# Projections turned before they leave the PSUM banks, stacks built by transfers through a scratch, keys and values by plain fp32 matmuls

## The reference, cut to what matters

```
Q = layernorm(x) @ Wq + bq ;  K = ctx @ Wk + bk ;  V = ctx @ Wv + bv
w = softmax(Q K^T * 0.25)               (32 heads, 4 of them share one key/value head)
x = x + tanh(g_xattn) * ((w V) @ Wo + bo)
x = x + tanh(g_ffn) * ffn(layernorm(x))     ffn: w1, w3 (512 -> 1792), silu, w2 (1792 -> 512)
```

## Time and profile before

| what | us |
|---|---|
| median of 3 runs (lowest to highest) | 392.64 (391.22 to 392.65) |
| the profiled execution: its own time | 391.85 |
| the profiled execution: span from first to last instruction | 390.1 |
| PE busy in the span | 377.4 |
| DVE, ACT, POOL busy in the span | 271.7, 209.1, 160.5 |

### The profile page before, as it was taken

How to read it: one execution, slowest core, us unless ns; L and a number is a source line. 1 busy time by engine, 2 the same in 40 slices (tenths; PEclk the granted TensorE clock), 3 DMA queues, 4 the chain that set the end, 5 groups by cost and what they waited for, 6 DMA issues and landing times.

```text
span 390.1 us, 6293 instructions
## 1 busy us (share of the span) xinstructions
PE 377.4 (97%) x2350; PEld 307.5 (79%) x2350; DVE 271.7 (70%) x452; ACT 209.1 (54%) x367; POOL 160.5 (41%) x135
## 2 busy tenths in 40 slices
PE   7789999999998999999999999999999999999996
PEld 5578888888887677878888888888888888888885
DVE  5978998979998967898776777543954344554334
ACT  4678999998999986552332332332332332332320
POOL 6558889898999785264333443000000000000000
PEclk9999999999999999999999999999999999999999
DMA  8903104100000040295000000000200000000002
GB/s 289 342 14 86 32 2 167 46 40 6 2 6 3 3 166 2 86 416 227 0 0 0 0 0 0 0 0 2 108 0 0 0 0 0 0 0 0 0 0 108
DMA packets 6817, 20.98 MB, mean 54 GB/s; under 512 B 875, under 2 KB 1131, under 8 KB 6668
## 3 DMA queue, kind: packets, MB, share of 16 engines
q1 hardware_dynamic: 6364, 19.92, 14.0%
q10 hardware_dynamic: 432, 0.79, 0.5%
HBM read 18.28 MB, written 2.10 MB: 52 GB/s over the span
## 4 chain that ended last, share of the span: by engine, by line
PE 83%; DVE 9%; DMA 3%; SPq 2%; ACT 1%; issue 1%; POOL 0%; DVEq 0%
PE ps L1767 23%; PE ps L1769 23%; PE ps L1768 22%; PE ps L1819 3%; PE ps L1809 3%; PE ps L1774 3%; DMA gsc<-in_small 3%; DVE MX L1142 2%; PE ps L1827 2%; PE ps L1775 1%; PE ps L1828 1%; DVE x2HL L1172 1%; DVE X L1183 1%; DVE aTL L1153 1%; DMA Qst<-Mrow 1%
## 5 line engine op out<-in xcount | busy, mean ns | idle before, releaser
L1767 PE MATMUL ps<-x2HL,w13H 128*128 128x512 f32 x224 | 89.1, 398 | 0.0
L1769 PE MATMUL ps<-x2HL,w13L 128*128 128x512 f32 x224 | 88.6, 395 | 0.0
L1768 PE MATMUL ps<-x2HL,w13H 128*128 128x512 f32 x224 | 88.4, 395 | 0.0
L340 POOL TENSOR_TENSOR PL<-E,PH 128x512 f16<-128x512 f32 x64 | 74.1, 1174 | 13.2 <-ACT E L609 7.2
L351 POOL TENSOR_TENSOR wres<-wres,gsc 128x1536 f32<-128x1536 f32 x14 | 42.5, 3037 | 44.2 <-DVE hf L1196 44.2
L632 ACT ACTIVATE T<-ps 128x512 f32<-128x512 f32 x28 | 16.7, 597 | 79.0 <-PE ps L1769 79.0
L640 ACT ACTIVATE hH<-hf 128x512 fp32r<-128x512 f32 x28 | 17.7, 632 | 63.5 <-DVE hf L1196 63.5
L1769 PEld LDWEIGHTS ps<-x2HL,w13L 128*128 128x128 f32 x224 | 42.0, 187 | 10.4
L1768 PEld LDWEIGHTS ps<-x2HL,w13H 128*128 128x128 f32 x224 | 42.0, 188 | 9.8
L1189 DVE SCALAR_TENSOR_TENSOR A<-T,ps 128x512 f32<-128x512 f32 x28 | 19.2, 685 | 43.8 <-ACT T L632 43.8
L1767 PEld LDWEIGHTS ps<-x2HL,w13H 128*128 128x128 f32 x224 | 42.0, 188 | 9.5
(11 more groups left out here) (112 smaller groups left out, 712.8 us busy)
## 6 DMA issues: line engine op xcount, KB each, us to landing
wres<-in_wff SPq DMA_DIRECT2D x14, 768.0 KB, 6.7
X<-in_x SPq DMA_DIRECT2D x8, 256.0 KB, 11.1
ct<-in_ctxt SPq DMA_DIRECT2D x7, 256.0 KB, 3.2
raw<-in_wproj SPq DMA_DIRECT2D x3, 512.0 KB, 6.3
out<-X SPq DMA_DIRECT2D x6, 256.0 KB, 2.0
raw<-in_wproj SPq DMA_DIRECT2D x1, 1024.0 KB, 9.4
Qst<-Mrow SPq DMA_DIRECT2D x32, 8.0 KB
out<-X ACTq DMA_DIRECT2D x2, 256.0 KB, 2.1
```

Of the source, the lines that this page charges most:

```text
L340: pool.tensor_tensor(PL[:, g % NL, :], E[:, g % NE, :], PH[:, g, :], ALU.subtract).then_inc(pL_ok, 1)
L1767: pe.matmul(out_ap, aH, bH, start=start, stop=False)
L1768: pe.matmul(out_ap, aH, bL, start=False, stop=False)
L1769: return pe.matmul(out_ap, aL, bH, start=False, stop=stop)
```

## The change

It does five things, and writes all five lists of operations anew.

1. **Keys and values** come from plain fp32 matmuls on the unsplit context `ct` and the unsplit weights `raw` (`project_kv32`): 4 matmuls of 256 columns for two batches at once, for K and for V each. The splits of the context (`context_high`, `context_low` on POOL) and of Wk, Wv are gone. The weights are the stationary operand, so that the result is turned: features on the partitions.
2. **Queries** too are made turned and for two batches at once: `project_q` for each j of 4, 4 x three matmuls of 256 columns.
3. **Biases** are then one value per partition and are added while the parts are written (`q_high`, `q_low`, `k_high`, `k_low`, `v_bias`); the bias matmuls are gone. V is turned back by `turn_v`.
4. **Stacks** are built by transfers: the high and low parts go to a scratch in device memory (`queries_out`, `keys_out`), and each of the three parts is read back from there to its 32 rows of `Qst` or `kst` (`queries_in`, `keys_in`). The 24 turns and 6 ACT copies per batch are gone. The score groups go by j instead of h, so `scores(n, j)` needs all four pairs.
5. **Maxima**: one transfer per batch (two for batch 0) into 16 rows, the sign moves into `sel`, `max_low` moves from DVE to POOL. The first layernorm's `normalise` moves from ACT to DVE (8), and 2 of the 8 of the second; some small steps (`epsilon`, `shift`) move to POOL, and the low part of Wq from DVE to POOL.

The diff, cut to its core:

```diff
-            def project_kv(n, bank, k):
-                project(bank, 2 * KVD, ctH[:, n % 2], ctL[:, n % 2], KV0, k)
-            def add_bias(bank, width, b0):
-                return pe.matmul(bank[:, 0:width], ones[:], brow[:, b0:b0 + width], start=False, stop=True)
-            def stack_k(h, bank):
-                for i in range(4):
-                    m = turn(bank[0:ROWS, i * P:(i + 1) * P], Ktok[...])
-            def stack_q(h, bank):
-                for j in range(GJ):
-                    m = turn(bank[0:ROWS, j * P:(j + 1) * P], Qtok[...])
+            def project_kv32(bank, n, w0, k0, k1):
...
+                for k in range(k0, k1):
+                    m = pe.matmul(bank[:, 0:TWO], raw[:, w0 + k * KVD:w0 + (k + 1) * KVD],
+                                  ct[:, n % NCT:n % NCT + 2, k * P:(k + 1) * P], start=k == 0, stop=k == KB - 1)
+            def project_q(bank, j, k0, k1):
+                for k in range(k0, k1):
+                    c = Q0 + (j // 2) * KB * TWO + k * TWO + (j % 2) * P
+                    w = slice(c, c + P)
+                    m = three(bank[:, 0:TWO], WpH[:, w], WpL[:, w], xTH[:, k, :, :], xTL[:, k, :, :], k == 0, k == KB - 1)
+            def turn_v(bank):
+                for b in range(2):
+                    m = turn(bank[:, b * P:(b + 1) * P], VT[:, b * P:(b + 1) * P])
```

```diff
+        qscr = nc.dram_tensor("qscr", [NBATCH // 2, 2, 2, P, GJ * P], F32).ap()
+        kscr = nc.dram_tensor("kscr", [NBATCH // 2, 2, P, 2, TWO], F32).ap()
+        def keys_out(eng, p, low):
+            eng.dma_start(kscr[p, low], r32((KTL if low else KTH)[:])).then_inc((kh_out, kl_out)[low], 16)
+        def keys_in(eng, p, t):
+            s = (NBATCH - NKST + 2 * p % NKST) * P
+            eng.dma_start(r32(kall(32 * t, 32 * t + 32)[:, :, s:s + TWO]),
+                         kscr[p, t % 2].rearrange("(r h) g n -> r (h g) n", h=PAIRS)).then_inc((k_in0, k_in1)[p % 2], 16)
+        def queries_out(eng, p, low, j0, j1, done):
+            eng.dma_start(qscr[p, low, :, :, j0 * P:j1 * P].rearrange("b r n -> r b n"),
+                         r32((QTL if low else QTH)[:, :, j0:j1, :]).rearrange("r b j q -> r b (j q)")).then_inc(done, 16)
+        def queries_in(eng, n, t, done):
+            eng.dma_start(r32(Qst[32 * t:32 * t + 32, n % 2, :, :]).rearrange("r h n -> r (h n)"),
+                         qscr[n // 2, t // 2, n % 2].rearrange("(r h) n -> r (h n)", h=PAIRS)).then_inc(done, 16)
+        def max_in(eng, n, j0, j1):
+            eng.dma_start(r32(Qst[ROWS:ROWS + NM, n % 2, :, j0 * P:j1 * P]),
+                         r32(Mrow[0:NM, j0 * P:j1 * P]).unsqueeze(1).broadcast_to([NM, PAIRS, (j1 - j0) * P])).then_inc(mrow_in, 16)
...
+            sp.wait_ge(ql_out, 32)
+            sp.wait_ge(st_ps, 8)
+            queries_in(sp, 2, 2, q_in0)
+            sp.wait_ge(qh_out, 32)
+            queries_in(sp, 2, 0, q_in0)
```

```diff
+            def q_high(bank, j):
+                act.activation(QTH[:, :, j, :], bank[:, 0:TWO].rearrange("p (b q) -> p b q", b=2), ACT.Identity,
+                               bias=biasT[:, BQ + j:BQ + j + 1]).then_inc(qT_H, 1)
+            def k_low(bank, gg):
+                r = slice(64 * gg, 64 * gg + 64)
+                dve.scalar_tensor_tensor(out=KTL[r, gg, :], in0=bank[r, 0:TWO], scalar=biasT[r, BK:BK + 1],
+                                         in1=r32(KTH[r, gg, :]), op0=ALU.add, op1=ALU.subtract).then_inc(kT_L, 1)
+            def normalise(n):
+                dve.tensor_scalar(xn[:], X[:, n, :], rs1[:, n % 2, 0:1], nb1[:, n % 2, 0:1], ALU.mult, ALU.add).then_inc(xn_ok_dve, 1)
```

More of the change, by code:

```diff
@@ L44 @@
 TOK = HT * P
+TWO = 2 * P
+NM = 4 * PAIRS
 W13 = 2 * KB * P
@@ L555, in _ @@
             root2(5)
+            scale(2)
             pool.wait_ge(ve2_ok, 7)
@@ new lines, in _ @@
+            x_high(2, W1)
+            act.wait_ge(ql_out, 16)
+            queries_part(act, 0, 2, 2, 4, q_in0)
+            act.wait_ge(r1_ok, 1)
+            v_second(0, W2)
+            select_rows(act, 3)
+            act.wait_ge(vt_ps, 2)
+            v_first(2, W0)
+            queries_in(act, 1, 2, q_in1)
+            act.wait_ge(r1_ok, 2)
+            v_second(2, W0)
+            queries_in(act, 1, 1, q_in1)
+            act.wait_ge(v_ps, 3)
+            v_bias(W1)
+            out_bias_in(act)
@@ L1272, in _ @@
-            v_residue(1, W0)
-            dve.wait_ge(qtokH, 2)
-            q_low(W1)
-            dve.wait_ge(s_ps, 4)
-            row_max(3)
-            dve.wait_ge(max_ok, 4)
-            max_high(0)
-            mean(3)
-            dve.wait_ge(mH_ok, 1)
-            max_low(0)
-            dve.wait_ge(mean1, 4)
-            epsilon(3)
-            v_second(1)
-            dve.wait_ge(xTH_ok, 3)
-            x_low(W0)
-            out_bias()
-            dve.wait_ge(s_ps, 5)
-            row_max(0)
+            dve.wait_ge(qT_H, 2)
@@ new lines, in _ @@
+            q_low(W1, 1)
+            dve.wait_ge(qT_H, 3)
+            q_low(W2, 2)
+            epsilon(3)
+            statistics(4)
+            dve.wait_ge(nb1_ok, 3)
+            normalise(2)
+            dve.wait_ge(qT_H, 4)
+            q_low(W0, 3)
+            dve.wait_ge(k_ps, 2)
+            dve.wait_ge(kl_out, 16)
+            k_high(W1, 0)
+            dve.wait_ge(kT_H_dve, 3)
+            k_high(W1, 1)
+            mean(4)
+            dve.wait_ge(kT_H_dve, 4)
+            k_low(W1, 0)
@@ new lines, in _ @@
+            q_low(W0, 0)
+            dve.wait_ge(s_ps, 6)
+            row_max(1, 1)
+            dve.wait_ge(kT_H_dve, 6)
+            k_low(W1, 0)
+            k_low(W1, 1)
+            mean(5)
+            dve.wait_ge(qT_H, 6)
+            q_low(W2, 1)
+            normalise(4)
+            dve.wait_ge(s_ps, 7)
+            row_max(1, 2)
+            dve.wait_ge(vt_ps, 3)
+            v_first(4, W2)
+            dve.wait_ge(qT_H, 7)
+            q_low(W0, 2)
+            dve.wait_ge(v1_ok, 1)
@@ L1312, in _ @@
-            x_low(W1)
-            dve.wait_ge(s_ps, 8)
-            row_max(3)
-            dve.wait_ge(max_ok, 8)
-            max_high(0)
-            dve.wait_ge(mH_ok, 2)
-            max_low(0)
+            dve.wait_ge(v_ps, 4)
+            v_bias(W0)
+            dve.wait_ge(nb1_ok_pool, 2)
+            dve.wait_ge(xT_ps, 5)
+            normalise(5)
+            mean(6)
+            out_bias()
             dve.wait_ge(pv_ps, 4)
             denominators(1)
-            mean(4)
-            dve.wait_ge(mean1, 5)
@@ L1811, in scores, with turn_max @@
+            def scores(n, j):
+                b = 0 if n == 0 and j % 2 else 2
+                for h in range(PAIRS):
+                    m = pe.matmul(ps[:, b + h // 2, (h % 2) * TWO:(h % 2 + 1) * TWO],
+                                  Qst[0:ROWS, n % 2, h, j * P:(j + 1) * P], kst(n)[0:ROWS, 2 * h:2 * h + 2, :],
+                                  start=True, stop=True)
                 m.then_inc(s_ps, 1)
-            def turn_max(k, bank):
-                for j in range(GJ):
-                    m = turn(bank[0:4 * PAIRS, j * P:(j + 1) * P], Mtok[:, j, :, :, :].rearrange("p h g t -> p (h g t)"))
+            def turn_max(bank, j0, j1):
+                for j in range(j0, j1):
+                    m = turn(bank[0:NM, j * P:(j + 1) * P], Mtok[:, j, :, :, :].rearrange("p h g t -> p (h g t)"))
```

2534 lines of the change are left out of this document (1205 added, 1329 removed).

## The result

The changed kernel takes 412.13 us (median of 4 runs, 411.46 to 417.39) against 391.94 before (4 runs beside it, 391.22 to 392.65): a ratio of 1.0545, 95% interval 1.0454 to 1.0635. The forecast was 386 with a range of 375 to 394. It was wrong in its sign.

The account below looks back on a forecast made before the run. No single engine was taken to bound the middle, where four lay within six points; PE was full behind it. 391.85 + 2 (first stage) - 8 (middle) + 0.5 (tail) = 386.3, said as 386 us, range 375 to 394.

Parts of the forecast that it names:

- The plain fp32 product: Keys and values on PE: 0.45 us per 256-column plain fp32 matmul, 14.4 us for the 32 added.
- PE's work: PE's total load falls by 11 us (10 to 19); in the middle 90 us by its steps, before 109.
- The engines of the middle: Middle stage busy times after the change: POOL fullest at 99 us, DVE 95, PE 90, ACT 84.
- The length of 108: Middle stage, taken between 105 and 112 from POOL's 99 us at 94% or 88% full: -8 us.
- the second view: Middle stage: 69 us within the eight batches plus 38 us of PE work between them, 107 together.
- The landing of a read: Reading a stack back from device memory takes 3.2 us after an issue of 0.6, in first stage and middle.
- rival C: Middle: reload loop of Qst takes 16.5 of 18.5 us; with landings of about 8.5, slower, 398 us; chance 0.10.
- The argument against rival C: Middle: new traffic of 3.8 MB per batch pair in 27 us is 140 GB/s, under the first stage's 198.
- The first stage: First transposed score at 35 us instead of 33.1, PE's work and the query chain ending together: +2 (-1 to +6).
- The tail: Behind the last transposed score: scale(2) and chunk 2's split wait behind the last weight_low, +0.5 us (0 to 2).
- A: The new order fits better: start 33 us, middle 97 to 101, whole time 375 to 379, said 377; chance 0.22.
- B: Gain given back at start (38 us) and joints, middle 112, tail +2: whole time 391 to 394 us; chance 0.10.

Follow-up runs that it names:

- experiments 11 and 9: Changed kernel, respectively with dummy matmuls where PE waits for reads, 410.59 us, and with the second turn of batch 0's maxima ahead of scores(1,0), 415.77 us.
- experiment 8: Changed kernel with two waits added on POOL, so scale(0) and scale(3) start only after DVE's normalise(6) and normalise2(7): 414.09 us (1.0539).

## Why the prediction was wrong, step by step

- **The plain fp32 product and PE's work: right.** The plain fp32 product measured 0.47 with its end (0.45 taken). With few bytes read, PE shows 99.5 in the middle, from 114.2 in the earlier trace rows: 15 less by the modelled busy time, where the steps gave 19. PE was not what the loss hung on.
- **The engines of the middle: near enough.** DVE 94.5 (95 said). ACT 85.9 (84 said, but 4 of these were issues of transfers, which the busy time does not count, so its work was put 6 too low). POOL 92.9 (99 said: Wo's low part, 4.6, ran ahead of the stage, the added bias pass of 1.3 is not there, and its small steps took 0.27, not 0.35). The length of 108 that followed is borne out by 106.5 when the reads are small, but in part by luck: the second view had 69 between the first and last transposed scores of the batches and 38 in the gaps, and with small reads these were 61.9 and 44.6.
- **The landing of a read, the step that failed.** "Read back (issue 0.6, 3.2)" and "landing 3.2" in the loop of rival C. 3.2 is the median of the 256 KB input tiles, most of which landed in quiet stretches, and 3.1 is what one read takes with the queues to itself. But three reads go out together, onto 32 rows each, beside keys, writes and 768 KB chunks: 5.2 us on the page, 5.2 to 6.3 on the chain of the middle, 7.6 and 8.6 on that of the first stage. The sum of -8 for the middle and +2 for the first stage both stand on this one term. By the prediction's own count the loop was 16.5 of 18.5 available at 3.2, so it was full at 5.2; "it decides from a landing of about 8.5" was set where the loss would reach 11 us, not where the gain stops. The other numbers of that rule don't fit together either: a landing of 8.5 gives an excess of 3.3 and so 10 us, not 3.8 and 11. The gaps between the batches took 51.8 instead of 38. PE waited 11.0 us for six reads, three times for each of the two buffers. The third buffer gives back 6.6 of the middle, the small reads 12.1; that the old release part by part would have hidden the landing is argued, no run has it.
- **The argument against rival C was an average.** 3.8 MB in 27 us is 140 GB/s, and the middle did show 133. But the chain waits for bursts: in 60 to 65 us the queues were at 297 GB/s and a share of 1.01. The chance of 0.10 for the true mechanism followed from that average.
- **The first stage: the largest term, +2 said (to +6 as its bound), +15.1 measured.** The prediction took the reads as latency (two trips) and gave the queues no load, although its own had a share of 0.57 there for inputs alone. Its path had scores(0,0) near 23, the second halves back near 26 and the first transposed score at 35; they came at 30.5, 37.7 and 48.2, and batch 1's read of 8.6 us, which its path did not hold, stood on the chain as well. Measured: 1.8 to 5.6 from the reads' bytes, 1.2 to 3.1 from the waits for the writes when there is room; 1.2 to 3.3 from late Wo and contexts, which overlaps with the first. At least 6.8 of the 15.1 are not taken apart, and their cause stays open: the written order around `statistics(3)` (15.1 us for its tile to land; new orders alone gained nothing) and the 26 us of PE work that now stand ahead (18 before) may be in it, and no run separates them. The half clock of 30 to 40 us and the order of scores(1,0) are the less likely: experiments 11 and 9 changed them and the stage stayed at 48.4 and 48.5.
- **The tail: +0.5 said (0 to 2), +2.2 measured.** The mechanism was in the text for the middle (`normalise` up to 1.2 more beside POOL). The price was too small: POOL's `scale` is 2.8 us long, not 1.2, and the pass waits for all of it. PE's waits for DVE there rose from 0.6 to 2.8 us, which is the 2.2. No run got them back: experiment 8 freed one pass and the next took its place. In the middle the same happened to `normalise(6)` (3.02 us).
- **Rivals.** A did not come; its sum is also 2 too high at one end, since a middle of 97 to 101 gives 373 to 377. B had the place (the start) and a price far too low; its text has the tail at +2 and its sum at +1. C had the mechanism and the sign, but only for the middle, and its 398 would have been 14 short. That the measured 412 is so far off comes for the larger part from the first stage, where no rival had more than +5 (the term's own bound was +6).

## What to carry to other kernels

A detour through device memory has to be priced as load on the queues in the stretch where it runs, not as the latency of one transfer in a quiet one: look at the DMA share of that window, add the new bytes, and take the landing from a stretch that is as busy. A buffer that was released in parts by an engine and is now refilled whole by a transfer may need one buffer more (it gave back 6.6 us here). Where several engines lie within a few per cent, taking 8 to 22% off each left the order of waits as the bound here, and moving transfers to an earlier place in a full queue gained nothing in the two runs that tried it.

## What the runs showed of the hardware that was not expected

- The same 256 KB read took 3.1 us alone, 4.7 as the last of three, and 5.2 to 8.6 on the chain among the kernel's traffic.
- A POOL pass over 1536 columns held not only DVE's tensor-scalar pass (2.88 and 3.02 us for 0.55) but, once it was moved, a low part with both inputs in SBUF as well (2.87 for 0.69).
- The clock fell to the lower of its two levels during or behind some of PE's waits for a read, not all: with the wait of 5.0 us in the first stage (0.50 from 30 to 36 us) and three of the six in the middle (those of 1.3, 2.2 and 2.3 us; 0.50 for most of 108 to 111, 129 to 131 and 139 to 145 us), while it stayed at 1.00 behind those of 1.9, 1.7 and 1.7. The middle's mean grant was 0.94, with dummy matmuls ahead of three reads 0.99, with small reads 1.00. What this cost was not told from nothing.
